# The last batch of the first self attention taken out of its loop, its output, norm and sends made tile by tile, and a different hand-over from the cross attention to the last stage

## What is computed

```
x = x + attn0(layernorm(x))      # 16 heads of 32, rotary embedding
x = x + experts(layernorm(x))    # each token goes to one of four experts,
                                 # its three matrices are all ctx_2048[e]
x = x + bit_mlp(layernorm(x))
x = x + attn1(layernorm(x))
x = x + xattn(layernorm(x), ctx, mask)     # cross attention; its delta is layer-normed
y = layernorm(x)
s = max(max|y| / 448, 1e-7)      # one number for the whole tensor
x = x + (y / s rounded to fp8) @ weight.T * weight_scale + bias
```

## Time and profile before

| what | us |
|---|---|
| median of 3 runs | 1781.85 (1776.4 to 1787.78) |
| the profiled execution, its own time | 1790.49 |
| its span in the trace | 1788.6 |
| PE busy | 1509.2 (84%) |
| DVE busy | 1259.1 (70%) |
| ACT busy | 888.4 (50%) |
| POOL busy | 552.8 (31%) |

### The profile page before, as it was taken

How to read it: one execution, slowest core, us unless ns; L and a number is a source line. 1 busy time by engine, 2 the same in 40 slices (tenths; PEclk the granted TensorE clock), 3 DMA queues, 4 the chain that set the end, 5 groups by cost and what they waited for, 6 DMA issues and landing times.

```text
span 1788.6 us, 27098 instructions
## 1 busy us (share of the span) xinstructions
PE 1509.2 (84%) x8774; PEld 585.6 (33%) x8775; DVE 1259.1 (70%) x1768; ACT 888.4 (50%) x1081; POOL 552.8 (31%) x448
## 2 busy tenths in 40 slices
PE   1789999999848993788688999999979999999928
PEld 1223323233226661344332323333222333323213
DVE  4587897878845556888367788787736777768675
ACT  1336272452622333788645546463746454554634
POOL 0535447453420004422232232323132232414120
PEclk9889999999969997899888999999989999999969
DMA  3710202102123446200030111102231120203002
GB/s 117 246 37 3 70 25 60 34 15 56 63 101 107 141 135 142 36 1 0 6 108 18 39 34 27 45 13 58 94 98 45 36 59 23 70 9 85 0 30 95
DMA packets 80861, 106.32 MB, mean 59 GB/s; under 512 B 14112, under 2 KB 51360, under 8 KB 80672
## 3 DMA queue, kind: packets, MB, share of 16 engines
q1 hardware_dynamic: 77216, 97.14, 18.5%
q0 software_dynamic: 3584, 8.39, 2.2%
HBM read 49.26 MB, written 18.35 MB: 38 GB/s over the span
## 4 chain that ended last, share of the span: by engine, by line
PE 40%; DVE 9%; issue 5%; ACT 5%; DMA 2%; POOL 1%; POOLq 0%; SPq 0%; DVEq 0%; ACTq 0%
PE ps L426 16%; PE ps L805 6%; PE ps L972 5%; PE ps L819 5%; PE ps L1872 2%; ACT arena L1113 2%; PE ps L1854 2%; DVE arena L1165 1%; PE ps L750 1%; PE ps L2188 1%; PE ps L776 1%; DVE arena L1405 1%; DVE stats L180 1%; DVE arena L2026 1%; DMA x<-sorted_y,place 1%
## 5 line engine op out<-in xcount | busy, mean ns | idle before, releaser
L1113 ACT ACTIVATE arena<-ps 128x1024 f32<-128x1024 f32 x384 | 372.8, 1024 | 118.2 <-PE ps L972 107.4
L1165 DVE TENSOR_REDUCE arena<-ps 128x2 f32<-128x1024 f32 x256 | 299.6, 1220 | 58.0 <-PE ps L750 57.8
L426 PE MATMUL ps<-xt,w 128*128 128x512 f16 (+1 forms) x1872 | 304.1, 313 | 19.8 <-DVEq L152 8.8
L805 PE MATMUL ps<-arena 128*32 128x512 f32 x1536 | 210.6, 621 | 14.8 <-DVE arena L1200 8.8
L972 PE MATMUL ps<-arena 97*128 97x512 f16 (+1 forms) x768 | 214.7, 395 | 9.6 <-ACT arena L1113 6.8
L426 PEld LDWEIGHTS ps<-xt,w 128*128 128x128 f16 (+1 forms) x1872 | 153.6, 100 | 161.5 <-issue 58.8
L426 PE MATMUL ps<-w,arena 128*128 128x512 f16 (+1 forms) x804 | 185.9, 381 | 12.6 <-issue 12.6
L1326 DVE TENSOR_TENSOR arena<-arena 128x1024 f32<-128x1024 f32 x128 | 173.6, 1396 | 13.4 <-PE ps L819 11.8
L1535 POOL TENSOR_TENSOR arena<-arena 128x512 f16<-128x512 f32 x96 | 115.9, 1209 | 168.8 <-ACT arena L1093 164.0
L1088 ACT ACTIVATE arena<-ps,arena 128x512 f32<-128x512 f32 x96 | 65.8, 687 | 182.8 <-PE ps L426 175.4
L1405 DVE TENSOR_SCALAR arena<-arena 128x1024 f32<-128x1024 f32 x128 | 106.7, 839 | 69.4 <-ACT arena L1113 68.7
(11 more groups left out here) (200 smaller groups left out, 2029.7 us busy)
## 6 DMA issues: line engine op xcount, KB each, us to landing
arena<-arena SPq DMA_DIRECT2D x576, 64.0 KB, 2.0
raw<-in_ctxT SPq DMA_DIRECT2D x8, 1024.0 KB, 5.6
raw<-in_ffn_parts SPq DMA_DIRECT2D x16, 512.0 KB, 3.6
sorted_x<-arena SPq DMA_DIRECT2D x1, 4864.0 KB, 27.4
arena<-sorted_x SPq DMA_DIRECT2D x19, 256.0 KB, 3.5
sorted_y<-arena SPq DMA_DIRECT2D x19, 256.0 KB, 2.1
out<-x SPq DMA_DIRECT2D x16, 256.0 KB, 2.0
x<-in_x SPq DMA_DIRECT2D x1, 3072.0 KB, 15.8
```

The costliest lines, as they stand in the source:

```text
L426: last = pe.matmul(out, left[l](cl[k]), right[r](cr[k]), start=start and k == 0 and a == 0, stop=stop and k == n - 1 and a == 2)
L805: last = pe.matmul(self.context(g)[HD * j:HD * (j + 1)], self.v[:, kb, HD * (HG * g + j):HD * (HG * g + j + 1)], self.p(u)[:, j * S:(j + 1 ...
L1113: act.activation(self.p(u)[:, 2 * h * S:(2 * h + 2) * S], flat(self.m.ps[:, 2 * h:2 * h + 2, :]), ACT.Exp, scale=SOFTMAX_SCALE).then_inc(s ...
L1165: v.tensor_reduce(self.mx[:, g % 2, j:j + 2, t:t + 1].rearrange("p h t -> p (h t)"), self.slot_banks(item, b), AX.X, ALU.max).then_inc(sel ...
```

## The change

**Loops.** In attn0 batches 1 and 2 stay in a loop; batch 3 is written out with constants on every engine (`first_of`, `of_last`, a third plan in `make_plan`). In xattn the last batch is written out on SP, ACT and DVE; PE keeps its loop.

**The heads of batch 3 of attn0.** The norm and the turning of batch 0 are gone. In their place ACT splits the experts' matrices 0, 1 and 2 behind units 9, 11 and 13 and DVE behind its additions of units 11, 13 and 15 (`SPLIT`). SP loads matrix 0 when batch 3's stacking is done, matrix 1 when POOL has seen the sends of batch 2 land (their buffer is the same), matrix 2 when the values are projected, matrix 3 when the first is split.

**Behind the heads.** `pe_last_out` finishes the output tile by tile. `dve_last_out` does for each tile: add, statistics, aggregation, and the norm of the tile before; POOL makes each tile's root and sends the tile before. DVE splits matrix 3 only when POOL has issued the last send.

**The end of xattn.** The last batch loads and splits the weight of the last stage in place of the unused context; SP loads the bias, and POOL splits it behind the context of the third group of heads. The peaks of the last batch are made tile by tile: ACT writes |x - mean|, DVE takes the largest of each tile and multiplies by the roots at the end. The largest over the partitions is made by two PE transposes with DVE between them; POOL's reduction is gone.

```diff
+    def pool_tile(self, g, b, i):
+        m = self.m
+        g.wait_ge(*self.at(self.moments, b * T + i + 1))
+        g.tensor_tensor(m.rstd[:, i:i + 1], m.mv[:, i, 1:2], m.eps[:, 0:1], ALU.add).then_inc(self.eps_added, 1)
+        g.wait_ge(*self.at(self.eps_added, b + i + 1))
+        g.tensor_tensor(m.rstd[:, i:i + 1], m.rstd[:, i:i + 1], m.mhalf[:, 0:1], ALU.pow).then_inc(self.rstd_ready, 1)
...
+        if last:
+            units = {u: kinds.replace("x", "") for u, kinds in units.items()}
...
+    SPLIT = (9, 11, 13)
+    def of_last(self, b):
+        return self.rope and isinstance(b, int) and b == NB - 1
...
+            weights = self.following.weights
+            weights.load(sp, 0)
             sp.wait_ge(*self.at(self.sent, NB - 1))
-        self.sp_following(sp)
-        if self.rope:
-            self.following.weights.sp_rest(sp)
-    def sp_batch(self, sp, b):
+            weights.load(sp, 1)
+            self.wait_full(sp, ("v", T - 1), NB - 1)
+            weights.load(sp, 2)
+            weights.sp_rest(sp)
...
+    def pe_last_out(self, pe):
+        pe.wait_ge(*self.at(self.cl, NB * C - 1))
+        for i in range(2):
+            self.pe_out(pe, i, range(C - 1))
+        pe.wait_ge(*self.at(self.cl, NB * C))
+        for i in range(2):
+            self.pe_out(pe, i, [C - 1]).then_inc(self.out_full, 1)
+        for i in range(2, T):
+            self.pe_out(pe, i, range(C)).then_inc(self.out_full, 1)
...
+    def act_sizes(self, act, b):
+        for i in range(T):
+            act.wait_ge(*self.at(self.ynorm.moments, b * T + i + 1))
+            act.activation(self.m.xn[:, i, :], slot(self.m.x, b * T + i), ACT.Abs, scale=-1.0,
+                           bias=self.m.mv[:, i, 0:1]).then_inc(self.ynorm.xn_ready, 1)
...
+            if self.of_last(b) and u in self.SPLIT:
+                self.following.weights.act(act, self.SPLIT.index(u))
             if self.cross and NH // 2 <= u < NH // 2 + C:
-                self.act_audio(act, b + 1, u - NH // 2)
+                if last:
+                    self.following.act_weight(act, u - NH // 2)
+                else:
+                    self.act_audio(act, b + 1, u - NH // 2)
...
+    def dve_last_out(self, v, b):
+        src, dst = (lambda i: slot(self.m.x, b * T + i)), (lambda i: self.normed_tokens(b)[:, i, :])
+        self.dve_places(v, b)
+        for i in range(T):
+            self.dve_out(v, i, b)
+            v.wait_ge(*self.at(self.out_added, b * T + i + 1))
+            self.ynorm.dve_tile_stats(v, b, i, src)
+            if i:
+                self.ynorm.dve_tile_apply(v, b, i - 1, src, dst)
+        self.ynorm.dve_tile_apply(v, b, T - 1, src, dst)
+        v.wait_ge(*self.at(self.sent, NB))
+        self.following.weights.dve(v, NE - 1)
...
+            if self.of_last(b):
+                if u - 2 in self.SPLIT:
+                    self.following.weights.dve(v, self.SPLIT.index(u - 2))
+            elif u == (3 if self.rope else 0):
...
+    def dve_last_peaks(self, v, b):
+        m = self.m
+        peaks = m.final_peak[:, NB - 1:NB - 1 + T]
+        def peak(i):
+            v.wait_ge(*self.at(self.ynorm.xn_ready, b * T + i + 1))
+            v.tensor_reduce(peaks[:, i:i + 1], m.xn[:, i, :], AX.X, ALU.max).then_inc(self.peak, 1)
+        for i in range(T):
+            xs = slot(m.x, b * T + i)
+            v.scalar_tensor_tensor(out=xs, in0=self.delta[:, i, :], scalar=m.rstd[:, i:i + 1], in1=xs,
+                                   op0=ALU.mult, op1=ALU.add).then_inc(self.x_done, 1)
+            v.wait_ge(*self.at(self.x_done, b * T + i + 1))
+            v.memset(m.carrier[:], 0.0)
+            self.ynorm.dve_stats(v, lambda i: slot(m.x, b * T + i), (i,))
+            v.wait_ge(*self.at(self.ynorm.sums, b * T + i + 1))
+            v.memset(m.carrier[:], 0.0)
+            v.bn_aggr(m.mv[:, i, :], m.stats[:, i, :]).then_inc(self.ynorm.moments, 1)
+            if i:
+                peak(i - 1)
+        v.wait_ge(*self.at(self.ynorm.moments, b * T + T))
+        v.tensor_copy(m.final_mean[:, b * T:(b + 1) * T], m.mv[:, :, 0:1].rearrange("p t a -> p (t a)")).then_inc(self.kept, 1)
+        v.wait_ge(*self.at(self.ynorm.rstd_ready, b + 1))
+        v.tensor_copy(m.final_rstd[:, b * T:(b + 1) * T], m.rstd[:]).then_inc(self.kept, 1)
+        peak(T - 1)
+        v.wait_ge(*self.at(self.peak, b + T))
+        v.tensor_tensor(peaks, peaks, m.rstd[:], ALU.mult).then_inc(self.peak, 1)
...
+            self.pool_self(g, NB - 1, False)
+            for i in range(T):
+                self.ynorm.pool_tile(g, NB - 1, i)
+                if i:
+                    self.pool_send(g, NB - 1, i - 1, i)
+            self.pool_send(g, NB - 1, T - 1, T)
+            g.sem_inc(self.sent, 1)
...
+    def pool_send(self, g, b, lo, hi):
+        m = self.m
+        g.wait_ge(*self.at(self.ynorm.xn_ready, b * T + hi))
         g.wait_ge(*self.at(self.place_ready, b + 1))
         g.wait_ge(*m.zero_filled)
-        g.tensor_tensor(self.pool_carrier, m.eps[:, 0:1], m.eps[:, 1:2], ALU.add)
-        for i in range(T):
+        g.tensor_tensor(self.pool_carrier[:, lo:lo + 1], m.eps[:, 0:1], m.eps[:, 1:2], ALU.add)
+        for i in range(lo, hi):
             g.indirect_dma_start(self.io["sorted_x"][:, :], bass.IndirectOffsetOnAxis(self.place_now[:, i:i + 1], 0),
                                  self.normed_tokens(b)[:, i, :], None).then_inc(self.scattered, 16)
...
+        pe.wait_ge(*self.at(self.peak, 1))
+        pe.transpose(m.ps[0:1, 7, 0:P], self.top[:, 0:1], m.ident[:]).then_inc(self.peak_turned, 1)
+        pe.wait_ge(*self.at(self.scale, 2))
+        pe.transpose(m.ps[:, 6, 0:1], self.row_peak[0:1, :], m.ident[0:1, 0:1]).then_inc(self.peak_turned, 1)
...
         v.tensor_reduce(self.top[:, 0:1], m.final_peak[:], AX.X, ALU.max).then_inc(self.peak, 1)
-        v.wait_ge(*self.at(self.whigh, 1))
-        v.scalar_tensor_tensor(out=flat(m.w[:, 0, 1]), in0=flat(m.raw[:, 0]), scalar=self.ws64,
-                               in1=flat(m.w[:, 0, 0]), op0=ALU.mult, op1=ALU.subtract).then_inc(self.wlow, 1)
-        v.wait_ge(*self.at(self.allred, 1))
-        v.tensor_scalar(self.top[:, 2:3], self.top[:, 1:2], 1.0 / 448.0, 1e-7, ALU.mult, ALU.max).then_inc(self.scale, 1)
+        v.wait_ge(*self.at(self.peak_turned, 1))
+        v.tensor_reduce(self.top[0:1, 1:2], m.ps[0:1, 7, 0:P], AX.X, ALU.max).then_inc(self.scale, 1)
         v.wait_ge(*self.at(self.scale, 1))
+        v.tensor_scalar(self.row_peak[0:1, :], m.ps[0:1, 7, 0:P], self.top[0:1, 1:2], None, ALU.max).then_inc(self.scale, 1)
+        v.wait_ge(*self.at(self.peak_turned, 2))
+        v.tensor_scalar(self.top[:, 2:3], m.ps[:, 6, 0:1], 1.0 / 448.0, 1e-7, ALU.mult, ALU.max).then_inc(self.scale, 1)
+        v.wait_ge(*self.at(self.scale, 3))
...
-    def pool(self, g):
-        g.wait_ge(*self.at(self.peak, 1))
-        g.partition_all_reduce(self.top[:, 1:2], self.top[:, 0:1], P, RMAX).then_inc(self.allred, 1)
+    def pool_parts(self, g):
+        g.wait_ge(*self.at(self.const, 16))
         g.memset(self.pick[0:96, :], 0.0).then_inc(self.pick_made, 1)
         g.wait_ge(*self.at(self.pick_made, 1))
         for k in range(3):
             g.memset(self.pick[32 * k:32 * k + 1, :], 1.0).then_inc(self.pick_made, 1)
         g.wait_ge(*self.at(self.pick_made, 4))
-        g.wait_ge(*self.at(self.const, 16))
```

213 lines of the change are left out of this document (130 added, 83 removed).

## The result

| | us |
|---|---|
| before, median of 4 runs beside it | 1783.82 |
| changed, median of 4 runs | 1756.73 (1750.91 to 1761.23) |
| ratio | 0.985, interval 0.982 to 0.987 |
| changed, the profiled execution's own time (span) | 1761.23 (1759.4) |
| before, the same | 1790.49 (1788.6) |

What follows compares the result with a forecast made beforehand. PE is busy 84% of the span, so time is gained only where it stands still. Terms -13.9 + 2.0 - 9.75 = -21.7 bring the profiled 1790.49 to 1768.8 and the median 1781.85 to 1760 us; range 1748 to 1774.

Steps and rivals of the forecast that it cites:

- Behind the heads, -13.9: From attn0's last output matmul to SP's first expert load: 23.25 us becomes 9.3; bounds -15.5 and -11.
- Matrix 3 is split on DVE behind the last issue: Behind attn0's heads: this split ends at 8.4 us, before the 9.3, hidden under the landing of the sends.
- The 48 output matmuls, 0: Attn0's output: same matmuls in tile order, last tile full 11.05 us after the start as before; no cost.
- The heads, +2.0: Batch 3 of attn0: norm gone -2.4, ACT's splits +3.2, DVE's splits +1.2; bounds -2.4 and +7.
- The splits are 4.4 as forecast: Heads of batch 3: three splits each on ACT and DVE, costing 3.2 and 1.2 us.
- The credit of 2.4 for the norm: Heads of batch 3: without batch 0's norm ahead of it, a DVE addition can start 2.4 us earlier.
- the heads pay more: Rival: ACT's and DVE's splits add up in chained waits, heads cost 7 us, total 1765; chance 0.15.
- The end of xattn and the last stage, -9.75: Second tile's matmuls start 9.75 us earlier, bias parts being ready; includes 1.9 from xattn's end; bounds -7.6 and -10.4.
- the largest over the partitions: End of xattn: two PE transposes with small DVE steps take about 2.4 us, before 2.84; -0.4, bounds -1.2 and +0.8.
- second tile as reckoned: Last stage: the eight matmuls of tile 1 start at 1740.9 instead of 1750.66.
- The step to 1760: Whole kernel: the steps' 21.7 us, taken as absolute, come off the runs' median of 1781.85.
- The rival of the shared port: Heads: POOL's low half of group three could wait for DVE, PE's output starting 1.5 us later; not taken, no chance given.

Runs made afterwards that it cites:

- e8: Changed kernel with a real POOL addition raising the semaphore for the fourth split: last output matmul to SP's load 9.23 us, in place of 10.5.
- e5: Changed kernel with the three splits cut to 8 columns (work left out): first exponential to first output matmul 51.90 us, in place of 56.3.
- e12: Changed kernel with bias parts made in the last stage, POOL also waiting for DVE's first rounding: xattn's end to PE's end 70.80 us; heads, unchanged code, 54.62.
- e10: Changed kernel with the bias parts made in the last stage, behind the largest |y|: xattn's end to PE's end 68.46 us, against 65.5 to 66.7.

## Why the prediction was right, and where it was not

The total came out because two errors met, which is luck. The places gave 16.7 in place of 21.7 us; the middle of the program, and what stays open, gave the rest.

- **Behind the heads, -13.9.** Measured -12.7. The chain of addition, statistics, root, norm and sends came to its sum within 0.1 once the semaphore waited for the send (e8). The failing step was "Matrix 3 is split on DVE behind the last issue": it was not behind it.
- **The 48 output matmuls, 0.** Measured +1.7. "The 48 are the same, so the last tile is full 11.05 us after the start" left out the clock. The longer wait for the last sum was in the prediction's own reckoning (the last addition ends later), and PE's pace behind it was not asked for.
- **The heads, +2.0.** Measured +3.5. The splits are 4.4 as forecast (e5), 0.9 of it by the clock of the last sum, which the forecast did not have; the shares of ACT and of DVE were not measured apart. The credit of 2.4 for the norm was the failing step: with the norm gone, POOL's list moved too, and its bias additions met DVE's additions at a worse time. The step was read from DVE's rows alone; of the step that was removed, the part on POOL was not followed. And the clock, which fell behind PE's waits, was not in the sum: up to 1.65 by e12. This is nearest to the rival "the heads pay more", whose reason (the two engines' splits add up) was wrong.
- **The end of xattn and the last stage, -9.75.** Measured -9.2 in the mean: -1.4 to the end of the peak (from the first output matmul at 1678.89 to 1706.22 are 27.33, before 28.69), the largest over the partitions -1.0 (forecast -0.4), second tile as reckoned. Both the size and the wait named hold: in before the bias parts held PE until 1746.02, and early parts free it. What the prediction did not ask is why they were so late. e10 and e12 put them back in their old place in the list and lose only 2 and 4 of the 6.8: there POOL starts on them 7.4 and 4.8 us sooner behind the peak.
- **From the profiled execution to the median.** The step to 1760 takes the 21.7 off the median of before, and that is sound. But of the profiled execution's 1790.49, 8.6 lay in the middle and were gone in the next trace, so that the 29.3 between the two profiled executions is no measure of the steps. The medians differ by 27.1 beside each other, and by 21.7 over the runs of both sessions; of either, 16.7 are accounted for.

The rival of the shared port did not come as a new wait: the low half of group three ran at once, 1.40 long, and PE did not wait for it. DVE's pair beside it took 3.31, as it did in before (3.32), where a pair alone takes 2.32; so this meeting costs the last sum 1.0 in both kernels. The Trainium skill, "SBUF — State Buffer", section "Who interferes with whom", says of another case, DVE's two-port modes, that whoever issues first gets the shared pair for the whole instruction and the other blocks. The prediction took the whole instruction over to two SBUF inputs beside a GpSimd read, of which the section says that they contend. The order does decide here: with DVE first POOL's four took 6.93 and DVE's pair 3.40, with POOL first 4.95 and 5.90. That one waits for the whole of the other's instruction is not what e12 shows, as far as POOL's rough spans can tell: POOL lost 0.3 us to one step of DVE, and the next two-input step of DVE (L2399) took 0.98 in place of 0.69 and ended at 1714.15, before POOL's at 1714.50. What such a meeting costs the program is found in the list of who waits for the stretched instruction: 3.6 us at the pair beside L1644, 5.0 by the first output matmul.

## What to carry to other kernels

When a step is removed from a list, everything behind it on that engine moves forward: look for what it now runs beside, on every engine that the step had a part on. A longer wait of PE has a second price, the slower clock behind it, and it can differ between executions of the same code. Where a wait means "issued", hang it on a real instruction behind the issue, not on a bare semaphore step. And a single pair of profiles can differ by more than the change in places that the change does not touch: compare the changed stretches, and take a second profile of the old kernel before explaining the rest.

## What was not expected of the hardware

- A semaphore raised by POOL's sequencer behind an indirect DMA is seen before that DMA is issued: DVE began at 508.95, the issue's row starts at 511.44. A real POOL instruction in its place was seen only behind it (e8).
- POOL's power step on one column of 128 takes 0.57; on four columns mostly 1.02, and 1.88 beside a DVE pair (446.17 in before).
- Four POOL additions of two SBUF inputs (4.95) beside one pair of DVE additions of two SBUF inputs (2.32 alone) stretch the pair to 5.90 to 6.15 when POOL is first; POOL's own four are then not longer than the 4.94 that they take alone. With DVE's pair 0.3 us ahead POOL's four take 6.93 and the pair 3.40.
- Behind the same wait of PE (2.8 us, then 3.9) the granted clock fell in five traces of the same code at both places, and in e12 at the second alone: 56.3 and 54.62 us for the heads.
- The batches of xattn took 48.1 or 49.7 from the first exponential to the last two in the same program; of the 56 batches in 14 traces none lies between.
